# Second expert layer: three doubled positions of gathered tokens become dense experts, four single gathered slots remain

## The reference

```python
logits = (x @ gate_w + gate_b) / 0.9
topk_vals, topk_idx = jax.lax.top_k(logits, 2)
keep = jax.nn.one_hot(topk_idx, 8, dtype=jnp.bool_).any(-2)
gate_probs = jax.nn.softmax(jnp.where(keep, logits, -jnp.inf))
h = jax.nn.gelu(jnp.einsum('bsd,edf->bsef', x, w1) + b1, approximate=False)
expert_out = jnp.einsum('bsef,efd->bsed', h, w2) + b2
out = jnp.einsum('bse,bsed->bsd', gate_probs, expert_out)
out = (out - mean(out)) / jnp.sqrt(var(out) + 1e-5) * ln_g + ln_b
```

## Time and profile before

| what | us |
|---|---|
| median of three runs | 2531.23 (2530.8 to 2531.26) |
| the profiled execution | 2532.78 |
| its span in the trace | 2531.0 |
| TensorE busy | 2498.1 (99%) |
| VectorE, ScalarE, GpSimd busy | 1960.8, 1853.0, 1168.3 |
| mean granted clock of TensorE | 0.998 |

### The profile page before, as it was taken

One profiled execution on the slowest core, in us unless ns is written; L12 is line 12 of the kernel. 1 busy time (PEld: TensorE's weight loads), 2 busy tenths in 40 slices (PEclk: granted clock), 3 DMA queues, 4 the chain that ended last, 5 costly groups with the idle time before them and its releaser, 6 DMA issues.

```text
span 2531.0 us, 53053 instructions
## 1 busy us (share of the span) xinstructions
PE 2498.1 (99%) x18030; PEld 2003.0 (79%) x18030; DVE 1960.8 (77%) x3724; ACT 1853.0 (73%) x6961; POOL 1168.3 (46%) x1925
## 2 busy tenths in 40 slices
PE   8999999999999999999999999999999999999998
PEld 6876999877777777777777777777777776688886
DVE  8886866687878787878787878787878787577668
ACT  2214444288888888888888888888888889456665
POOL 5433211255565556565555555565556553320000
PEclk9999999999999999999999999999999999999999
DMA  9995544566776676667766766677677667245564
GB/s 389 385 374 216 193 184 171 151 169 163 169 176 160 163 177 161 166 164 170 176 157 165 176 162 165 165 168 177 155 170 167 165 145 208 111 183 199 187 229 143
DMA packets 138031, 472.96 MB, mean 187 GB/s; under 512 B 32664, under 2 KB 32792, under 8 KB 126368
## 3 DMA queue, kind: packets, MB, share of 16 engines
q1 hardware_dynamic: 130512, 456.20, 64.4%
q10 hardware_dynamic: 7248, 13.37, 1.4%
HBM read 244.53 MB, written 17.30 MB: 103 GB/s over the span
## 4 chain that ended last, share of the span: by engine, by line
PE 95%; DVE 2%; ACT 1%; DMA 1%; issue 0%; POOL 0%; SPq 0%; DVEq 0%; ACTq 0%
PE PB L801 21%; PE PB L831 15%; PE PB L819 14%; PE PB L842 14%; PE PB L761 6%; PE PB L607 6%; PE PB L1011 4%; PE PB L1038 4%; PE PB L774 3%; ACT EE L1236 1%; PE PB L650 1%; PE PB L941 1%; PE PB L952 1%; DMA AR<-in_ctx 1%; PE PB L1019 1%; PE PB L707 1%
## 5 line engine op out<-in xcount | busy, mean ns | idle before, releaser
L1236 ACT ACTIVATE EE<-PB,small 128x256 f32<-128x256 f32 x3136 | 1438.0, 499 | 203.4 <-DVE small L1669 195.5
L1669 DVE TENSOR_REDUCE small<-PB 128x2 f32<-128x512 f32 x1568 | 1028.3, 683 | 313.8 <-PE PB L831 310.1
L1236 ACT ACTIVATION_READ_ACCUMULATOR EE<-PB,small 128x1 f32 x3136 | 724.3, 231 | 0.0
L831 PEld LDWEIGHTS PB<-QS,STK 128*128 128x128 f32 x3136 | 557.7, 188 | 175.3 <-issue 42.4
L801 PE MATMUL PB<-CTX,WKV 128*128 128x512 f32 x2352 | 681.2, 394 | 0.0
L2067 POOL TENSOR_TENSOR VS<-V,small 128x128 f32<-128x128 f32 x784 | 332.5, 424 | 674.1 <-DVE small L1675 674.0
L831 PE MATMUL PB<-QS,STK 128*128 128x256 f32 x3136 | 617.5, 286 | 3.1 <-ACT EE L1236 3.0
L819 PE MATMUL PB<-WKV,CTX 128*128 128x512 f32 x1584 | 468.8, 393 | 0.0
L801 PEld LDWEIGHTS PB<-CTX,WKV 128*128 128x128 f32 x2352 | 385.1, 189 | 29.5
L842 PE MATMUL PB<-EE,VS 128*32 128x256 f32 x6272 | 367.5, 381 | 1.0 <-POOL VS L2067 1.0
L2054 POOL TENSOR_TENSOR CTX<-RAW,CTX 128x256 fp32r<-128x256 f32 x384 | 284.0, 740 | 20.5 <-DVE CTX L1605 20.5
(11 more groups left out here) (290 smaller groups left out, 2477.3 us busy)
## 6 DMA issues: line engine op xcount, KB each, us to landing
STK<-KHL SPq DMA_DIRECT2D x1568, 128.0 KB, 2.4
RW<-in_l1f SPq DMA_DIRECT2D x64, 1024.0 KB, 5.6
AR<-in_ctx SPq DMA_DIRECT2D x49, 1024.0 KB, 8.3
RAW<-in_ctx SPq DMA_DIRECT2D x98, 512.0 KB, 3.8
WF<-in_l0f SPq DMA_DIRECT2D x17, 2304.0 KB, 8.9
V<-v_scr SPq DMA_DIRECT2D x64, 256.0 KB, 3.0
v_scr<-RAW ACTq DMA_DIRECT2D x49, 256.0 KB, 7.5
RW<-in_l1a SPq DMA_DIRECT2D x1, 4096.0 KB, 13.5
```

The source lines that it names most:

```text
L831: m = e.matmul(bank(2 * (k % 2) + half, 256 * (s % 2), 256), STK[:, g % 2, s, c % 2, j:j + 128], QS[:, s, c, :], start=True, stop=True)
L1236: m = e.activation(EE[:, b, s, :], bank(2 * (k % 2) + half, 256 * (s % 2), 256), ACT.Exp, bias=nm[:, b, s:s + 1], accum_out=su[:, b, s:s + 1])
L1669: e.tensor_reduce(nm[:, k % RING, 2 * half:2 * half + 2], bank(2 * (k % 2) + half).rearrange("p (s i) -> p s i", s=2), axis=AX.X, op=ALU.m ...
```

## The change

Four experts are computed dense instead of one: expert 0, as before, and the experts at positions 0, 1 and 2, to which VectorE's sorting now brings those with over 128 tokens. The other four positions have one slot each. So there are 64 dense chunks (`ND`) over 16 pieces of weights (`NPC`), then four slots of four quarters (`NQ` = 16), and two pairs of slots instead of five. The dense experts take turns on the banks 4, 5 and 6, 7; their biases and weights in the sum come from `B1O` and `wt_o`, and `add1` for the first three runs within the dense loop. The transfers of the 32 pieces are the same in size and number; the pieces from the fifth on are chosen by a number that SP reads from the sorted table. Both pairs of places are made at chunk 16, and the first gather moves to chunks 60 and 61. The diff, cut to its core:

```diff
-NPC = 4
+FULL = 4
+NPC = 4 * FULL
+ND = 16 * FULL
 EXPERTS = 7
-SLOTS_OF = ((0, 1), (2,), (3, 4), (5,), (6, 7), (8,), (9,))
-SLOTS = 10
-SEQ = [(s, x, q) for x in range(EXPERTS) for q in range(4) for s in SLOTS_OF[x]]
-NQ = len(SEQ)
+SLOTS = 8 - FULL
+NQ = 4 * SLOTS
 PAIRS = SLOTS // 2
+GATHER = {8 * p - 5 + z: (p, z // 2, z % 2) for p in range(1, PAIRS) for z in range(4)}
+TURN_PLACE = {4 * s + 2: s for s in range(SLOTS)}
+RESULT = {4 * s + 6: s for s in range(SLOTS)}
...
+            def load_up(n):
+                if n >= 4 and n % 4 == 0:
+                    x = n // 4 - 1
+                    w.wait_ge("r_tab", 1)
+                    expert.append(e.value_load(EI[0:1, x:x + 1], min_val=0, max_val=7))
+                    e.dma_start(B1O[:, x, :], a["l1g"][:, bass.ds(expert[x] * 16, 16)]).then_inc(S["d_b1o"], 16)
+                if n >= 3:
+                    w.wait_ge(*raw_read(n - 3, 0))
+                e.dma_start(RW[:, n % 3, 0:2048], piece(n, 0)).then_inc(S[f"d_p{n % 3}"], 16)
...
             def down1(n, i):
...
+                if fc == 0 and x == 1:
+                    w.wait_ge("b2_out", 2)
+                if fc == 0 and x >= 2:
+                    w.wait_ge("f1_acc", 2 * (x - 2) + i + 1)
...
-            for n in range(16):
+            for n in range(ND):
                 up1(n)
...
-                if n in (12, 13):
+                if n in (ND - 4, ND - 3):
                     for cc in range(2):
-                        gather(0, n - 12, cc, 6 + cc)
+                        gather(0, n - ND + 4, cc, 4 + cc)
...
+                if x:
+                    w.wait_ge("d_b1o", 16 * x)
                 e.activation(HF1[:, n % 4, :], bank(n % 4, 0, 256), ACT.Gelu,
-                             bias=b1[:, n:n + 1]).then_inc(S["f1_gelu"], 1)
+                             bias=B1O[:, x - 1, f:f + 1] if x else b1[:, f:f + 1]).then_inc(S["f1_gelu"], 1)
...
             for m in range(-1, NQ + 1):
-                if m in CAST_DOWN:
-                    cast_down(CAST_DOWN[m])
+                if 0 <= m - 1 < NQ:
+                    cast_down(m - 1)
...
-                if m in CAST_UP:
-                    cast_up(CAST_UP[m])
+                if m + 2 < NQ:
+                    cast_up(m + 2)
...
-                done(e.tensor_tensor(rest, num, before, ALU.subtract))
-                e.tensor_scalar(least, rest, 2.0, 1.0, ALU.mult, ALU.add).then_inc(seq.sem, seq.up())
-                done(e.tensor_scalar(rest, rest, -2.0, 12.0, ALU.mult, ALU.add))
-                done(e.tensor_tensor(least, least, rest, ALU.min))
-                done(e.scalar_tensor_tensor(out=rest, in0=before, scalar=2.0, in1=least, op0=ALU.mult, op1=ALU.subtract))
-                done(e.tensor_tensor(rest, rest, ov, ALU.mult))
-                done(e.tensor_tensor(rest, rest, least, ALU.add))
+                done(e.tensor_scalar(rest, num, -1.0, 6.0, ALU.mult, ALU.add))
+                done(e.scalar_tensor_tensor(out=rest, in0=ov, scalar=1.0, in1=rest, op0=ALU.subtract, op1=ALU.mult))
+                done(e.tensor_tensor(rest, before, rest, ALU.subtract))
...
-                if n == 11:
-                    place(0)
+                if n == 16:
+                    for p in range(PAIRS):
+                        place(p)
+                if n == 11:
...
                 if n // 4 + 1 < NPC and n % 4 in (1, 2):
                     split1(n // 4 + 1, n % 4 - 1)
-                if n == 14:
+                if n >= 2 and (n - 2) % 16 == 15:
+                    for i in range(2):
+                        add1((n - 2) // 16, i)
+                if n == ND - 2:
                     rest_up(0)
```

More of the change, by code:

```diff
@@ L535, in load_down, with piece @@
[L535 to L540, removed]
+            expert = []
+            def piece(n, h):
+                if n < 4:
+                    return a["l1f"][n][:, 2048 * h:2048 * h + 2048]
+                x = expert[n // 4 - 1]
+                return a["l1f"][bass.ds(x * 4 + n % 4, 1), :, 2048 * h:2048 * h + 2048].rearrange("o p f -> (o p) f")
@@ L542, in sync_program, with load_down @@
+            def load_down(n):
+                if n >= 3:
+                    w.wait_ge(*raw_read(n - 3, 1))
+                e.dma_start(RW[:, n % 3, 2048:4096], piece(n, 1)).then_inc(S[f"d_w{n % 3}"], 16)
+            def load_piece(n):
+                load_up(n)
+                load_down(n)
             w.wait_ge("d_s1", 256 * NPAIR)
@@ L553, in sync_program @@
             load_piece(2)
[L554 to L561, removed]
+            for n in range(3, NPC + 2):
+                load_piece(n)
+            load_up(NPC + 2)
+            for n in range(NPC + 3, 32):
                 load_up(n)
                 load_down(n - 1)
-            load_down(PIECES - 1)
+            load_down(31)
             for i in range(2):
@@ L1314, in gather_out @@
                 w.wait_ge("ga_mm", 4 * p + 2 * h + cc + 1)
-                if p >= 2:
-                    w.wait_ge("u_mm", SLOT_LAST[2 * p - 3] + 1)
                 e.activation(XG[:, p % 2, h, 2 * cc:2 * cc + 2, :], bank(b).rearrange("p (c j) -> p c j", c=2),
                              ACT.Copy).then_inc(S["ga_out"], 1)
-            for n in range(16):
+            for n in range(ND):
                 gelu(n)
@@ L1788, in kept_and_combined @@
                 e.tensor_tensor(comb1, t3, sv.unsqueeze(2).to_broadcast([P, 2, 8]), ALU.mult).then_inc(S["g1_comb"], 1)
-            ov, before, rest, least, num = (small[:, o:o + 7] for o in (176, 184, 192, 200, 208))
+            ov, before, rest, num = (small[:, o:o + 7] for o in (176, 184, 192, 208))
             t77, oh = (small[:, o:o + 49].rearrange("p (a b) -> p a b", a=7) for o in (216, 272))
@@ L1832, in slot_tables @@
                 done(e.tensor_reduce(wt_o, pick, axis=AX.X, op=ALU.add))
[L1833 to L1837, removed]
+                e.tensor_copy(RQ[:, :, :], rk_o[:, :, FULL - 1:EXPERTS]).then_inc(seq.sem, seq.up())
+                done(e.tensor_copy(CWT[:, :, :], wt_o[:, :, FULL - 1:EXPERTS]))
             def place(p):
-                if p >= 2:
-                    w.wait_ge("pt_mm", 2 * (p - 2) + 2)
                 for z in range(2):
@@ L1917, in vector_program @@
                     for i in range(2):
-                        add1(0, i)
+                        add1(FULL - 1, i)
                 if m in RESULT:
                     result(RESULT[m])
-                if m - 1 in CAST_UP:
-                    rest_up(CAST_UP[m - 1])
-                if m in CAST_DOWN:
-                    rest_down(CAST_DOWN[m])
-                if m in PLACE:
-                    place(PLACE[m])
+                if m + 1 < NQ:
+                    rest_up(m + 1)
+                if 0 <= m - 1 < NQ:
+                    rest_down(m - 1)
                 if 0 <= m - 1 < NQ:
@@ L1936, in add_slots @@
                     w.wait_ge("f1_half", 1)
-                w.wait_ge("f1_acc", 2)
-                e.tensor_tensor(ACC[:, i, :], ACC[:, i, :], bank(4 + i), ALU.add).then_inc(S["f1_acc"], 1)
+                w.wait_ge("f1_acc", 2 * FULL)
+                e.tensor_tensor(ACC[:, i, :], ACC[:, i, :], bank(6 + i), ALU.add).then_inc(S["f1_acc"], 1)
             def y(i):
```

114 lines of the change are left out of this document (46 added, 68 removed).

## The result

The changed kernel takes 2509.49 us (median of four runs, 2509.08 to 2512.1) against 2531.02 us before (2530.17 to 2531.26), a ratio of 0.9918 with a 95% interval of 0.9901 to 0.9935. The forecast was 2509.8 us. In a later set it was 2509.8 against 2531.12 us (ratio 0.9915, 0.9902 to 0.9929). So 21.3 to 21.5 us are gone, and 21.5 were forecast.

A forecast was written before the change was run, and what follows sets the result against it. TensorE's own stream was taken as the bound, busy for 99% of the span. 135.4 - 141.8 - 5.5 - 5.5 - 4.1 = -21.5 us, from 2531.2 to 2509.7, put down as 2509.8 us; range 2507.5 to 2517.

The forecast's parts named there:

- The dense chunk, 2.82 us: TensorE's time per dense chunk, from starts; 48 chunks added, 135.4 us.
- The quarter, 5.91 us: TensorE's time per plain quarter of a slot, from starts; 24 quarters removed, 141.8 us.
- The helpers, 15.1 us: TensorE work removed with six slots: gathers 5.5 us, scatters 5.5 us, turned places 4.1 us.
- The dense form against the quarters, 6.4 us: On TensorE, 135.4 us added against 141.8 removed; 0.54 us per piece, eight transposes less what shorter matmuls lose.
- Cover of 2.2 us in the dense chunks: Time between GpSimd's low part of hidden values and its TensorE consumer; sums push 1.5 us into it, costed at nothing.
- VectorE's slack in the quarters: In single quarters VectorE takes 5.8 of 5.91 us, slack counted in tenths; cost 0, bounds 0 and 8 us.
- rival 2: VectorE becomes the bound of the 16 single quarters, 0.5 us in each: 2517.7 us; chance 0.06.
- rival 3: Weights arrive too late in the run of single quarters, 58 us at 193 GB/s: 2568 us; chance 0.02.
- rival 4: The clock falls in the 48 added dense chunks, +135 us: 2645 us; chance 0.01.

The follow-up runs named there:

- `turns_twice`: The changed kernel with each quarter's four transposes made twice: 2516.42 us.
- `low_on_pool`: The changed kernel with the low part of the hidden values of the 16 quarters made by GpSimd instead of VectorE: 2509.24 us against 2509.8.
- `eight_slots`: The kernel before with one doubled position instead of three, so eight slots instead of ten: 2479.82 us against 2531.18.
- `after_again`: The changed kernel run once more, unedited, in a later set: 2509.8 us.
- `dense_dve1`: The changed kernel with one more VectorE subtraction of 128x1024 in each of the 12 added dense pieces: 2514.99 us.
- `more_dma512`: The changed kernel with one more transfer of 512 KB beside each of the last 13 pieces of weights: 2509.64 us.
- `more_dma1024`: The changed kernel with one more transfer of 1024 KB beside each of the last 13 pieces of weights: 2518.79 us.

## Why the prediction was right

The forecast of 21.5 us held to within 0.2 us in the medians, and the mechanism was the one forecast: fewer us in TensorE's own stream, with nothing beside it in the way. That the medians agree so closely is in part luck: a comparison tells about 4 us, and each short stretch at half the clock, there in some executions of either kernel, is worth 1.5 us. The traces are the better witness. From the start of chunk 9 to the end of the last quarter, with no stretch at 0.50 in either, the kernel before takes 284.4 us and the changed one 262.8, 21.6 us less. Its steps, one by one:

- **The dense chunk, 2.82 us.** Held in all 48 added chunks.
- **The quarter, 5.91 us.** Held. The path was TensorE's alone in the changed kernel, as `turns_twice` (7 us more for work on it) and `low_on_pool` (nothing for work beside it) show.
- **The helpers, 15.1 us.** Part of a gather 0.45 (6.36), scatter and turned places 7.51 together: the same as in the earlier trace rows, within 0.01 us. `eight_slots` shows that they are paid in full.
- **The dense form against the quarters, 6.4 us.** The sum was right: 2.82 and 5.91 us were both kept. Its explanation by two parts, transposes saved and shorter matmuls lost, has only an estimate for their sizes, 10.8 and 4.3 us.
- **Cover of 2.2 us in the dense chunks.** Too simple, though nothing came of it: 1.2 us remained behind the sums, where I had 0.7, but a delay of 1.2 us there came out as 2.5, with GpSimd's subtraction at 2.98 us instead of 1.65. At six of the nine other pieces the three added subtractions, 3.4 us by their starts, cost 1.1 us each, so 2.3 us of cover were there; at the other three they cost 2.5 us.
- **VectorE's slack in the quarters.** Mis-sized, since the distance of starts held a wait: 0.9 us per slot, where I had next to none. It cost the forecast nothing, as VectorE's share was put at 0; but rival 2 was further away than I said.
- **Transfers (rival 3).** Away by a margin that is now measured: 322 GB/s used of 415 to 420.
- **The clock (rival 4).** The added chunks ran at 1.00 throughout, with up matmuls of 256 columns, as the row of before had it. But the profiled span fell by 20.6 us and not 21.5, and here the clock did come in. Chunks 7 and 8 of the changed kernel, TensorE:

```profile
2229.19 1.81 PE L932 MATMUL PB<-XS,WSB 128*128 128x256 f32 x12
2230.80 2.76 PE L947 MATMUL PB<-WSB,HS 128*128 128x512 f32 x6
2233.36 1.89 PE L932 MATMUL PB<-XS,WSA 128*128 128x256 f32 x12
...
2236.47 1.60 PE L932 MATMUL PB<-XS,WSA 128*128 128x256 f32 x12
```

The six matmuls at 2230.80 take 2.56 us to the next start, where 1.39 are usual; with the chunk after it 1.5 us are lost, in the stretch at 0.50 behind the product with b2 (four matmuls with eight partitions), where TensorE had not been idle. The other such stretch, at chunk 5 behind the wait of 0.87 us, is in the profiled executions of both kernels. So the expert layer shrank by 20.0 us in the two traces (315.3 to 295.2 us from the first up matmul to the end of the last quarter), and 21.5 without the second stretch; another 0.6 us came from ahead of the layer, where nothing was changed.

## What to carry to other kernels

When one engine's stream is the time, price both forms by the distance between starts of whole repeating units, count units, and the sum can come out within a few per cent, as here; prices of small groups inside a unit need an experiment that doubles them. Gathering pays only where it saves more columns than its helpers and transposes cost: two slots of 128 tokens are all 256 tokens, and the dense form needs neither. Before pushing an instruction into a gap beside GpSimd, look at what VectorE runs then: the gap that the trace shows isn't the gap that is left.

## What I had not expected of the hardware

- The clock falls or doesn't at the same place behind the same work. At chunk 5, behind a wait of 0.87 us and the routing's small matmuls, the granted clock was 0.50 for some 3 us in five profiled executions (the kernel before, the changed kernel, `after_again`, `dense_dve1`, `more_dma512`) and stayed 1.00 in the seven others that have this wait. Behind the product with b2, with no wait, it fell in two of the fourteen (the changed kernel and `dense_dve1`), and not in `after_again`, which is the changed kernel's own program. It is worth 1.5 us each time. Why it falls in one execution and not in another stays open.
- A GpSimd subtraction of 128x256 takes 0.74 us alone and 1.65 or 2.98 us beside VectorE's subtractions of 128x1024, and VectorE's get longer too (3.36 us for two instead of 2.35).
- With the added transfers of `more_dma512` and `more_dma1024`, weights came in at 414 and 419 GB/s over some 42 us.
